# Masked attention: who writes the mask of head 1 into its score bank in odd key tiles

## The reference, cut to what matters

```python
def _L1_xattn_ref(q, k, v, mask, wq_w, wq_b, wk_w, wk_b, wv_w, wv_b, fo_w, fo_b):
    ...
    energy = jnp.einsum('nqhd,nkhd->nhqk', qp, kp)
    energy = jnp.where(mask == 0, jnp.float32(-1e+20), energy)
    attention = jax.nn.softmax(energy / np.float32(np.sqrt(EMBED)), axis=3)
    out = jnp.einsum('nhql,nlhd->nqhd', attention, vp).reshape(N, -1, EMBED)
    return out @ fo_w.T + fo_b
```

## Time and profile before

| | |
|---|---|
| median of 3 runs | 2099.51 us (2098.49 to 2099.77) |
| profiled execution, first to last instruction | 2122.9 us |
| its first 1100 us (before the masked attention) | PE busy 1053.9 us |
| masked attention | about 1101 to 1885 us |
| a group of the masked attention | 45.1 to 55.4 us |
| PE busy in all / DVE / ACT / POOL | 93% / 60% / 42% / 25% |

### The profile page before, as it was taken

One profiled execution on the slowest core, in us unless ns is written; L12 is line 12 of the kernel. 1 busy time (PEld: TensorE's weight loads), 2 busy tenths in 40 slices (PEclk: granted clock), 3 DMA queues, 4 the chain that ended last, 5 costly groups with the idle time before them and its releaser, 6 DMA issues. The chain is left out here.

```text
span 2122.9 us, 27241 instructions
## 1 busy us (share of the span) xinstructions
PE 1982.3 (93%) x10186; PEld 1100.5 (52%) x10186; DVE 1269.1 (60%) x2541; ACT 893.8 (42%) x1791; POOL 528.3 (25%) x454
## 2 busy tenths in 40 slices
PE   7989999999999999899989999999999999965994
PEld 5666567745676567746643333433433343334773
DVE  5423765366633764367777777777776777741343
ACT  3412211221112211121118888778777977841221
POOL 4311000210001000000034223236324531426664
PEclk9999999999999999999999999999999999986997
DMA  8743000110001000110226383345335432215986
GB/s 286 213 200 111 1 1 11 45 43 1 1 21 62 1 1 11 34 28 16 44 79 129 85 259 81 80 120 123 90 70 146 104 57 43 73 62 164 251 182 157
DMA packets 101531, 184.97 MB, mean 87 GB/s; under 512 B 38151, under 2 KB 62549, under 8 KB 100120
## 3 DMA queue, kind: packets, MB, share of 16 engines
q1 hardware_dynamic: 83000, 153.24, 26.8%
q0 software_dynamic: 18400, 30.00, 6.3%
HBM read 127.38 MB, written 65.25 MB: 91 GB/s over the span
## 5 line engine op out<-in xcount | busy, mean ns | idle before, releaser
L2216 DVE CUSTOM_DVE_ANT_0 ps<-ps,maskN 128x801 f32<-128x801 f32 x480 | 467.7, 1014 | 129.5 <-PE ps L2009 126.3
L2189 ACT ACTIVATE d_prob<-ps 128x512 f32<-128x512 f32 (+1 forms) x832 | 473.4, 597 | 158.3 <-PE ps L2039 153.2
L856 PE MATMUL ps<-vx_or_keys,b_xT 128*128 128x512 f32 x512 | 240.3, 597 | 4.9 <-DVE val_or_prob L1209 4.9
L840 PE MATMUL ps<-oxB,og_or_pT 128*128 128x256 f32 x1024 | 241.1, 380 | 0.0
L2051 PE MATMUL ps<-d_prob,vaug 128*32 128x512 f32 (+1 forms) x1664 | 226.6, 610 | 0.3 <-ACT d_prob L2189 0.3
L840 PEld LDWEIGHTS ps<-oxB,og_or_pT 128*128 128x128 f32 x1024 | 190.5, 190 | 37.4 <-issue 11.2
L2038 PE MATMUL ps<-maskT,identb 128*128 128x512 bf16 (+1 forms) x498 | 192.2, 386 | 5.7 <-DVE d_oN L2248 1.7
L1095 ACT ACTIVATE prob_or_gate<-ps,b_mx 128x512 f32<-128x512 f32 (+3 forms) x128 | 66.1, 525 | 289.4 <-DVE b_mx L1200 289.4
L2185 ACT CAST ps<-maskT 128x512 f32<-128x512 bf16 (+1 forms) x310 | 185.6, 599 | 0.0
L260 POOL DMA_INDIRECT table<-xr,slot x128 | 128.6, 1005 | 177.5 <-PE ps L2039 140.8
L1209 DVE TENSOR_TENSOR val_or_prob<-ps,b_gm 128x512 f32<-128x512 f32 x128 | 88.4, 691 | 107.1 <-PE ps L856 107.0
(11 more groups left out here) (321 smaller groups left out, 2807.8 us busy)
## 6 DMA issues: line engine op xcount, KB each, us to landing
c_rawT<-in_maskT SPq DMA_DIRECT2D x24, 512.0 KB
vx_or_keys<-k_parts SPq DMA_DIRECT2D x60, 200.1 KB, 7.2
k_parts<-x_k SPq DMA_DIRECT2D x16, 600.4 KB
table<-xr POOLq DMA_DIRECT2D x16, 578.0 KB
e_buf<-table SPq DMA_DIRECT2D x32, 289.0 KB
raw<-in_mask SPq DMA_DIRECT2D x10, 800.5 KB, 4.2
vx_or_keys<-in_D_w SPq DMA_DIRECT2D x12, 640.0 KB, 5.5
e_w<-in_D_w SPq DMA_DIRECT2D x12, 640.0 KB
```

Of the source, the lines that this page charges most:

```text
L840: mm = pe.matmul(ps[:, 6 + t // 2, (t % 2) * D:(t % 2 + 1) * D], og[:, e, t * P:(t + 1) * P], oxB[:, p, e, :], start=first and t % 2 == 0, ...
L856: mm = pe.matmul(ps[:, bank, :], xTB[:, c, t * P:(t + 1) * P], vxB[:, c, h, :], start=c == 0, stop=c == NC - 1)
L2189: nc.scalar.activation(prob[0:w, T % 2, h, :], ps[0:w, BANKS[GH * T + h], :], ACT.Exp, scale=SCALE_C).then_inc(exped, 1)
L2216: v.tensor_tensor_reduce(banks, banks, maskN[:, t, MO[half]:MO[half] + w], 1.0, -3.0e38, ALU.add, ALU.max, mp[:, t, h, half:half + 1]).the ...
```

## The change

In the odd tiles of groups 0 to 14 the mask of head 1 comes from DVE in place of PE, where the bank allows it. The plan gives "dve" for `i % 2 and h == 1`; this holds in 90 scores (6 odd tiles by 15 groups): the plan's 498 masks of PE become 408, its 24 of DVE become 114, and the 310 of ACT, all the banks and all that frees them stay as they are. PE's part is already written for it: such a score waits for `mask_v` and issues L2039 alone.

On DVE the copy is placed after the maxima u = 1, 7, 13, 19, 25 and 31, for the tiles 1, 3, 5, 7, 9 and 11: in the middle of the maxima that PE issues in the tile before. It waits for the bank and, in groups with g = 0, for the mask's tile.

```diff
                     if i >= 1 and G == NGB - 1 and h % 2:
                         by = "dve"
+                    elif i % 2 and G < NGB - 1 and h == 1:
+                        by = "dve"
                     elif i >= 1 and G < NGB - 1 and h >= 2:
                         by = "act"
...
+            def mask_for(G, i, h):
+                u = GH * (NKT * G + i) + h
+                if MASKS[u][0] == "dve":
+                    bank_free(v, FREE[u])
+                    if G % NG == 0:
+                        v.wait_ge(biasT, NKT * (G // NG) + i + 1)
+                    v.tensor_copy(ps[0:KW[i], BANKS[u], :], maskT[0:KW[i], i, :]).then_inc(mask_v, 1)
...
                 for u in range(NM):
                     if G + 1 < NGB:
                         maximum(G + 1, u)
+                        if u % 6 == 1:
+                            mask_for(G, u // 3 + 1, 1)
                     if g == 2 and u % (NM // NT) == NM // NT - 1 and b + 1 < NB:
                         bias_n(b + 1, u // (NM // NT))
...
                 i, h = divmod(u - GH * NKT * (NGB - 1), GH)
-                if MASKS[u][0] == "dve":
-                    bank_free(v, FREE[u])
-                    v.tensor_copy(ps[0:KW[i], BANKS[u], :], maskT[0:KW[i], i, :]).then_inc(mask_v, 1)
+                mask_for(NGB - 1, i, h)
```

## The result

The changed kernel takes 2142.13 us (median of 4 runs, 2139.51 to 2144.91), the kernel before beside it 2099.64 us (2098.49 to 2103.68): ratio 1.0198, 95% interval 1.0183 to 1.0212. That is 42.5 us slower, where 31.5 had been forecast. Repeated on two other chips the same comparison gave 1.0180 [1.0148, 1.0212] and 1.0186 [1.0166, 1.0207], 35.7 and 38.4 us.

The account below looks back on a forecast made before the run. PE was taken to bound the kernel, with DVE close behind. Tile costs of +34.2 us, +3.8 for DVE's chains and -7.0 given back make +31.0, from 2099.5 to 2130.5, stated as 2131 us; range 2112 to 2152.

Parts of the forecast that it names:

- the whole gain that can be had: On PE, the bounding engine: removing 90 mask matmuls of 0.22 us each saves 19.8 us at most.
- rival 1: DVE's copy is hidden, so the 90 matmuls go and nothing is added: 2080 us; chance 4%.
- The interval, 2.21 us: From PE's second maximum to score 1 of the odd tile: DVE lag 0.54, maximum 0.92, copy 0.695, PE start 0.05.
- the full tiles: 28 odd tiles where PE now takes 1.56 us from second maximum to score 1: +0.65 us each, 18.2 us.
- the 2.00 us tiles: 23 odd tiles where a job stands between second maximum and score 1: +0.21 us each, 4.8 us.
- Tile 11: 12 tiles with a 1.22 us interval, where ACT already binds: taken at +0.40 us each, 4.8 us.
- the seven tiles taken at -0.22: Tiles where a longer job makes the interval 2.8 us or more, so only the matmul is saved: -1.5 us together.
- DVE's chains in groups with g = 1: Tiles 7, 8 and later, after the first such group: copies in DVE's routing steps add some 0.4 us each, 6 x 0.4.
- What is given back: DVE's DMA waits in groups 0 and 2 vanish, and the clock's drop with them: 2 x (1.8 + 1.7) = -7.0 us.
- Rival 2: PE's clock falls to 1.2 GHz for 3.4 us behind each new stall in 28 full tiles: +48 us, 2178; chance 7%.
- Nothing given back: DMA waits stay or shift with PE and tile 11 costs its full 0.99 us: +45 us, 2145; chance 10%.
- The plan changes little: Few of the scores have an admissible bank, so the time stays; chance 1%.

Follow-up runs that it names:

- kernel without masks: Kernel before with the mask matmul of head 1 left out in the 90 odd-tile scores, nothing in its place: 2122.01 us, 0.9986.
- S11: Not a run: masked-attention time summed over groups 1, 3, 4, 5, 7, 8, 9, 11 to 14; kernel before 545.8 us, changed kernel 576.4 to 576.5.
- the copies alone: Kernel before plus 90 DVE copies at the change's places into an unread SBUF buffer, PE keeping its masks: 2131.07 against 2124.61 us, 1.0027.
- the mask in tile 11: Kernel before with head 3's mask of tile 11 moved from ACT to DVE behind the last maximum, groups 0 to 14: 2127.97 against 2127.99 us, 0.9996.
- the run in which PE waits: Kernel before plus 90 DVE copies into an unread buffer, PE waiting for each ahead of its own mask matmul: 2158.74 against 2124.61 us, 1.0169.
- The kernel with the maximum first: Changed kernel with PE's first maximum of an odd tile moved ahead of score 1: 2149.79 us, 1.0114 against the kernel before.

## Why the prediction was right, point by point

The sign, the mechanism and the size were those of the prediction, and 2142.1 lies in its range; the centre was 11 us too low.

- **The bound, and whose heels DVE is on.** Right, but the prize was not. The prediction took the matmuls' 19.8 us as "the whole gain that can be had", and rival 1 priced itself by it. The kernel without masks shows 7 us in S11, of 14.5 by that reckoning. The order of time in which PE "had no stall" hides that the maxima and ACT's copies would stop it 0.1 us on. The forecast didn't rest on this, as it was made from the interval to score 1 and not from the sum of PE's work.
- **The interval, 2.21 us.** Measured 2.25: 0.54, 0.92 and the start with the accumulator's read (the first of the two bounds for it) were as read; the copy directly behind a maximum took 0.73 in place of the 0.695 of the earlier trace rows, and PE's start 0.06 in place of 0.05. That makes +0.69 or +0.70 in the full tiles for +0.65.
- **The classes.** What a tile cost is the time between the first scores of two tiles in a row, after less before; it repeats to 0.02 us in the three profiles. Tile 1 +0.48 (predicted 0.43), the 2.00 us tiles +0.26 (0.21). Group 7 went from 45.14 to 48.61 us (48.2). Tile 11 was taken too low: it cost +0.42, or +0.65 in groups 4 and 8, and another 0.19 follows in tile 12 in each of the 8 groups, together 0.61 and 0.84 for the 0.40 taken. PE in group 7, tiles 11 and 12:

```profile
1510.39 0.39 PE L2041 MATMUL ps<-vx_or_keys 99*128 99x512 bf16 x1 [1.08 <-DVE ps L2282]
...
1512.41 0.38 PE L2041 MATMUL ps<-vx_or_keys 99*65 99x512 bf16 x1
1512.79 0.41 PE L2040 MATMUL ps<-maskT,identb 65*65 65x512 bf16 x1
```

The last mask comes 0.38 us behind the score ahead of it, where the kernel before needed 0.22: ACT, which got score 1 of tile 11 late, takes the exponential out of that bank from 1512.14 on and needs 0.6 us for it. Of the seven tiles taken at -0.22, tile 11 in groups 1, 5 and 9 gave it (0.00 there and -0.21 in tile 12, as in the kernel without masks), but three of tile 9 gave +0.16; why was not looked into. DVE's chains in groups with g = 1 cost 0.59 or 0.60 a tile: near the 0.61 and 0.70 taken in five of six, but tile 7 of group 13 had been taken at 1.05. Tile 3 in g = 2 cost 0.38, where 0.66 was taken.
- **In sum.** For the 11 groups the prediction's terms make 25.8 us; measured were 30.6 (32.0 in the first profile, below). Of the 4.8 missing, 0.05 in 46 tiles makes 2.3, tiles 11 and 12 make 2.1, the three tiles 9 1.1, and DVE's chains take 0.8 off. For the other five groups the terms make +5.2 us, measured +3.2, on executions that differ by more than that.
- **What is given back.** The wait of group 0 (1.75, 2.12 and 2.09 us in the kernel before) is gone in all three profiles of after, and its tile 10 is 1.90 shorter. That of group 2 is 0.94, 0.44 and 0.56 us and did not go as predicted; in the kernel before it is 1.85, 0.36 and 2.87, so one execution does not tell what the change gives back there, and 3.5 us for it was too much to count on; this row is its rest (DVE, group 2) and answers to the earlier trace rows:

```profile
1239.17 1.00 DVE L2272 TENSOR_SCALAR maskN<-raw 128x1601 bf16<-128x1601 int32 x1 [0.94 <-DMA raw<-in_mask]
```

No profile of after has the drop of the clock in group 2, which two of three of the kernel before have. Engines by stretch (as the earlier trace rows), which answers to the first of the earlier trace rows:

```profile
1236.00:1240.00 4.00, 3.84 (x23) 1.25 (x20) 2.84 (x5) 3.81 (x8) 4.00 (x7) 1.00 1.01 418
```

- **The clock.** Rival 2 would have cost 48 us more. Behind 82 of the 83 new waits the granted clock stayed at 1.00, those of 0.74 us in group 2 included (the row above). It fell once, behind one of the two longest, 1.32 us, in tile 11 of group 4. PE's row, and the stretch behind it:

```profile
1352.84 0.39 PE L2041 MATMUL ps<-vx_or_keys 99*128 99x512 bf16 x1 [1.32 <-DVE ps L2282]
```

```profile
1353.40:1356.80 3.40, 3.40 (x13) 0.82 (x6) 0.29 (x2) 2.12 (x5) 0.00 (x0) 0.51 0.00 0
```

This is the lower level, 1.2 GHz, for 3.4 us, and costs 1.4: the reason for 577.8 in place of 576.4. In the two other profiles the same wait of 1.32 us was followed by 1.00. In the second the clock fell elsewhere, in a new wait of 2.09 us in tile 9 of group 10. The Trainium skill, "TensorE: Matmul & The Clock Gate", "A second HAM failure mode: psum-queue depth-cycling", would have had the clock swing with such frequent short stops; by that rule the prediction had 2178. The trace doesn't bear it out for stops of 0.9 us, and shows one case in three at this place for 1.32.
- **The other rivals.** The copy hidden (2080): fell, since 83 tiles wait. Nothing given back (2145): by its number the closest, but its mechanism isn't what happened, as tile 11 cost 0.61, tile 12 included, and not 0.99, and group 0's wait is gone. The plan changes little: fell, L2040 has 90 instructions fewer (408 in place of 498, read in the third profile of after; the first lacks 71 of its records).
- **What stays open.** The masked attention explains 34.3 us. The three comparisons give 42.5, 35.7 and 38.4, with intervals of some 3, 7 and 4 us to either side; the second holds 34.3. The stage ahead is equal, and the stage behind shows no difference beyond its spread, once its wait is taken off (before 221.9, 222.7, 220.4; after 225.7, 221.2, 218.8). So between 1 and 8 us of the timed difference are not placed in a stage by the mean of the profiles. Timed and profiled sums part by a few us in the small experiments too: the copies alone cost 3.3 us in S11 and 6.5 in the time, the mask in tile 11 saved 2.1 and 0. What does this was not tried; profiled executions alone show an order of time.

The masked attention as a whole was forecast at +31.0 us and measured at +34.3. What the sum had too small is the interval (0.05 a tile), the end of a group behind a late score 1 of tile 11, and three tiles 9. Two errors in part cancel in it: the 11 groups came out 4.8 us above their terms, the five others 2.0 below. The remaining 8 of the 11 us have no place in the traces.

## What to carry to other kernels

Before a matmul is replaced by another engine's copy, measure on the trace the interval from PE's last instruction that this engine must have worked off to the one that will wait: lag, work ahead, the copy and the hand-over, here 0.54 + 0.92 + 0.73 + 0.06 us against 1.56. Follow the late work to the end of the group: what is lost at a wait can grow where another engine binds. An engine that is only 60% busy can still be the wrong one, if it follows the bounding engine directly: its free time lies where it waits for that engine, and not where the new work is due. And a matmul of 0.22 us taken from an engine busy throughout gave 0.09 us, because the pair of banks that it writes next was still being read; take the matmuls out altogether first, and see what they are worth.

## What the runs showed of the hardware

- **Copies by DVE into SBUF were longer only beside POOL's work.** bf16 to f32, 128x512: 0.42 us in all 54 cases in which POOL's trace shows nothing beside it (and 0.42 to 0.43 in all 57 such cases of the run in which PE waits); of the 36 others 18 lasted 0.42 too, 17 lasted 0.46 to 0.74 us, 16 of these beside `maskT` (L1916), and one 3.10 (the row of L2286 above). Two such rows of the unread copies, beside POOL and without it:

```profile
1469.55 0.72 DVE L2286 CAST scratch<-gp 128x512 f32<-128x512 bf16 x1
```

```profile
1576.69 0.42 DVE L2286 CAST scratch<-gp 128x512 f32<-128x512 bf16 x1
```

The copy into PSUM was 0.73 us in all 90 places of after, 46 of them beside POOL's work. The Trainium skill, "VectorE: DVE Perf Modes", "Why PSUM operands drop a tier", says that a PSUM operand excludes the mode that reads one tensor through both SBUF ports. The two lengths agree with it; no run here changed the mode by itself.
- **A wait of one length doesn't settle the clock.** 1.32 us at the same place of the same program: the clock at 0.51 behind it once, at 1.00 twice. The kernel with the maximum first has 1.32 us at this place too, and 0.50 behind it.
- **The same program differs by 20 to 29 us between chips** (before 2099.6, and 2124.0 to 2128.8; after 2142.1, and 2162.4 to 2164.5). Kernels were therefore set only against runs on their own chip.
